# The end of a fused perceiver layer: a block closed without GpSimd's drain, and SyncE's last waits moved behind a branch

## The reference

```python
x = x + cross(layernorm(x), ctx_768)      # cosine of two projections, 256 wide
x = x + attention(layernorm(x))           # 16 heads of 16, each output freed of its share along v
x = x + experts(layernorm(x))             # top-1 of 14 experts, 256 -> 512 -> 256, gelu, times the probability
```

## Time and profile before

| what | value |
|---|---|
| median of three executions | 509.92 us (509.88 to 630.88) |
| span of the profiled execution | 518.2 us |
| instructions | 14215 |
| TensorE busy | 495.9 us, 96% of the span |
| GpSimd busy | 246.1 us, 47% |
| mean granted clock of TensorE | 0.992 |

### The profile page before, as it was taken

The page is one execution under the profiler, slowest core; times in us unless marked ns, Lnnn a source line. Parts: engine busy times, 40 slices in busy tenths (PEclk is TensorE's granted clock), DMA queues, the critical chain, the costliest instruction groups (busy, mean ns, idle before and its releaser), DMA issues.

```text
span 518.2 us, 14215 instructions
## 1 busy us (share of the span) xinstructions
PE 495.9 (96%) x4278; PEld 397.8 (77%) x4279; DVE 335.8 (65%) x1027; ACT 335.0 (65%) x814; POOL 246.1 (47%) x432
## 2 busy tenths in 40 slices
PE   8999999999999999999999999999879999999992
PEld 6545554667888888888888887778769999999992
DVE  4476665657889999888988899984632333323231
ACT  3766666589888988888888888764523333343430
POOL 2468665354334664655556555625443233333332
PEclk9999999999999999999999999999989999999998
DMA  8959995500002223222221122174545766666520
GB/s 302 311 173 282 304 259 172 168 1 3 2 2 72 67 74 92 92 51 88 92 92 46 46 63 69 44 250 145 183 167 186 220 208 209 220 192 212 187 82 8
DMA packets 35681, 70.41 MB, mean 136 GB/s; under 512 B 6752, under 2 KB 22242, under 8 KB 35632
## 3 DMA queue, kind: packets, MB, share of 16 engines
q1 hardware_dynamic: 31744, 60.72, 38.7%
q0 software_dynamic: 3456, 8.85, 4.5%
q10 hardware_dynamic: 432, 0.26, 0.2%
HBM read 58.93 MB, written 11.61 MB: 136 GB/s over the span
## 4 chain that ended last, share of the span: by engine, by line
PE 82%; DVE 5%; issue 4%; ACT 3%; POOL 2%; another core or an unknown queue 2%; DMA 1%; DVEq 0%; SPq 0%; POOLq 0%; ACTq 0%
PE psum L1520 11%; PE psum L1533 10%; PE psum L1446 9%; PE psum L1425 6%; PE psum L1404 6%; PE psum L1412 5%; PE psum L1475 5%; PE psum L1272 5%; PE psum L1372 5%; PE psum L1334 3%; PE psum L1343 3%; PE psum L1291 3%; PE psum L1294 3%; PE psum L1347 3%; PE psum L1312 2%
## 5 line engine op out<-in xcount | busy, mean ns | idle before, releaser
L1520 PEld LDWEIGHTS psum<-arena,ring 128*128 128x128 f32 x640 | 77.5, 192 | 4.6 <-ACT arena L1205 2.2
L1520 PE MATMUL psum<-arena,ring 128*128 128x128 f32 x640 | 78.5, 276 | 1.6 <-ACT arena L1205 1.5
L1533 PE MATMUL psum<-w_s,arena 128*128 x320 | 77.5, 386 | 0.0
L1205 ACT ACTIVATE arena<-psum 128x256 f32<-128x256 f32 x40 | 15.4, 385 | 94.0 <-PE psum L1272 53.0
L1021 DVE TENSOR_TENSOR arena<-psum,tok 128x256 f32<-128x256 f32 x40 | 17.0, 425 | 90.1 <-PE psum L1533 83.0
L1533 PEld LDWEIGHTS psum<-w_s,arena 128*128 128x128 f32 x320 | 58.7, 193 | 6.8
L545 POOL TENSOR_TENSOR ov<-o_n,v_s 128x256 f32<-128x256 f32 x32 | 26.1, 816 | 77.1 <-DVE o_n L785 77.1
L1171 ACT ACTIVATE arena<-kT,head_mask 128x256 f32<-128x256 f32 x128 | 59.3, 532 | 0.0
L603 POOL DMA_INDIRECT out<-arena,token_of x40 | 39.8, 996 | 19.7 <-POOL token_of L595 14.5
L1211 ACT ACTIVATE arena<-psum,b_s 128x128 f32<-128x128 f32 x160 | 45.6, 375 | 3.8 <-PE psum L1520 2.2
L892 DVE TENSOR_REDUCE smax<-psum 128x16 f32<-128x1024 f32 x32 | 39.1, 1222 | 11.4 <-PE psum L1425 11.3
(11 more groups left out here) (206 smaller groups left out, 1093.5 us busy)
## 6 DMA issues: line engine op xcount, KB each, us to landing
ring<-w SPq DMA_DIRECT2D x40, 512.0 KB, 3.6
w_s<-ctxT SPq DMA_DIRECT2D x15, 768.0 KB, 8.9
w_s<-w SPq DMA_DIRECT2D x16, 448.0 KB, 3.4
slot_rec<-routed SPq DMA_DIRECT2D x40, 132.0 KB
tok<-x SPq DMA_DIRECT2D x16, 256.0 KB, 8.2
w_s<-xT SPq DMA_DIRECT2D x12, 256.0 KB, 6.0
routed<-pad_rec SPq DMA_DIRECT2D x1, 1980.0 KB, 8.9
tok<-b SPq DMA_DIRECT2D x14, 128.0 KB
```

What stands on the lines that cost most here:

```text
L1520: mm = pe.matmul(hid_bank(p)[:, f * P:(f + 1) * P], w1_s[:, r, c * F + f * P:c * F + (f + 1) * P], xgT[:, p, c * P:(c + 1) * P], start=c = ...
L1533: mm = pe.matmul(bank(2 + q, D), hidT[:, q, f * P:(f + 1) * P], w2_s[:, bass.ds(e * (FC * D) + f * D, D)], start=f == 0, stop=f == FC - 1)
```

## The change

```diff
-        block = ctx.enter_context(nc.Block())
+        block = ctx.enter_context(nc.Block(no_gpsimd_drain=True))
...
+            def outputs_landed(slots):
+
+                for t in range(slots - 4, slots):
+                    sp.wait_ge(y_out[t % 4], arrivals(t, t % 4, 4, 16))
+
...
-                if isinstance(i, int) and i == part[1] - 1:
-
-                    for t in range(i - 3, i + 1):
-                        sp.wait_ge(y_out[t % 4], arrivals(t, t % 4, 4, 16))
+                if isinstance(i, int) and i == NSLOT - 1:
+                    outputs_landed(NSLOT)
...
             run_slots(sp, load_slot, 0, 0, used_tab, 1)
+            outputs_landed(EVEN)
```

## The result

The changed kernel takes 506.61 us (median of six executions, 506.08 to 506.88). The kernel before, beside it, takes 510.16 us (median of six; five lie between 509.88 and 510.24, one is the 630.88 us). 506.0 had been forecast. The medians differ by 3.5 us. The ratio is 0.9923, with a 95% interval of 0.991 to 0.9936, which stands for 3.9 us and 3.3 to 4.6. Run again on another chip with its variants, the changed kernel took 507.38 us against 510.64, ratio 0.9942 (0.9925 to 0.996).

What follows compares the result with a forecast made beforehand. Only the program's end was taken to matter, where the barrier waited for GpSimd's drain. 3.2 us from the drain and 0.7 from the branch made 3.9, so 509.92 - 3.9 = 506.0 us, with a range of 504.9 to 510.1.

Steps and rivals of the forecast that it cites:

- The view: End of the program: the closing line, not an average, shows the last 6.35 us, where nothing counts as busy.
- The drain, 3.2 us: Closing barrier: of GpSimd's 6.03 us drain, 2.8 us lie beside SyncE's wait and branch; removing it gains the exposed 3.2 us.
- The branch, 0.7 us, and nothing on its own: SyncE's load and branch after its last wait: moving the waits behind them gains 0.7 us, only with the drain gone.
- The small terms: Closing: 0.1 us from SyncE's last wait to its drain, 0.25 us for the new barrier (bounds 0.2 and 0.4).
- Carrying it over: From profiled execution to measured time: the 3.9 us was taken over as it is, 509.92 to 506.0 us.
- the 2% that I had set: Measured time: about 2% (10 us) was taken as what a measurement of this kernel can tell from no change.
- rival A: Behind the block: the drain's work comes back outside the span, or the option leaves the drain; 509.9 us, chance 0.16.
- the 8.3 us between span and median: Profiled execution: its span of 518.2 us stood 8.3 us above the median; the share due to profiling was left open.
- Rival C: Closing drain: long only because profiled, so less or only the branch's 0.7 us is gained; 506.8 to 509.2 us, chance 0.13.
- Rival B: Behind the block: winding-up starts only on request, and the closing there asks for it, taking 6.03 us; 512.2 us, chance 0.05.
- Rival D: Last outputs: they land sooner after issue when nothing is recorded; at most 6.0 us gained, 503.9 us, chance 0.05.

Runs made afterwards that it cites:

- the late drain: Kernel before, with GpSimd waiting for the last four outputs to land before its closing drain; 513.71 us against 510.57, ratio 1.0052.
- the kernel with the copy ahead of the wait: Changed kernel, with GpSimd copying the next slot's row numbers before waiting for output rows in slots 36 to 39; ratio to the kernel before 0.9946.
- the first four experiments: Variants of the kernel before: option alone (0.9951), moved waits alone (0.9999), one more drain ahead of the closing one (0.9999), GpSimd awaiting last outputs before draining (1.0052).
- the one with GpSimd's wait: Changed kernel, with GpSimd instead of SyncE waiting for the outputs of slots 36 to 39 to land; ratio to the kernel before 0.9932.

## Why the prediction was right

**The view.** The chain of waits ended at GpSimd's last scatter and showed nothing of the last 6.35 us. The closing line did, and all of the gain was in it. This held.

**The drain, 3.2 us.** Right in place and size: the option alone took the end of the span from 4.2 to between 1.1 and 1.2 us behind the last landing, where 3.1 had been expected of it, and 2.7 us off the median, with 1.7 to 3.3 inside its interval.

**The branch, 0.7 us, and nothing on its own.** Right. Moved alone it gave 0.9999; on top of the option the span's end drew in from 4.0 to 3.4 us behind the start of the last scatter. This is shown in the traces alone.

**The small terms.** I had 0.1 us from SyncE's last wait to its drain and 0.25 us for the barrier. It was 0.2 (504.2 to 504.4, one branch of 38 ns between) and 0.3 (504.4 to 504.7). The 0.25 us was charged for the new barrier, whose form no row of the kernel before shows; the changed kernel's closing has a drain on all engines but GpSimd as before, and one more semaphore instruction of 17 to 51 ns on each of the four. The last landing came 2.95 us after the scatter's start where it had been 3.05, which made up for most of it. So 3.9 us in the trace was right, partly by luck of 0.1 us or so, which is no more than these rows resolve.

**Carrying it over.** Here the sum had its largest error. I took 3.9 us over to the metric as it is. The new closing costs 0.3 us behind the span, which leaves 3.9 - 0.3 = 3.6 us. The medians differ by 3.5 us, but the interval of the ratio, 3.3 to 4.6 us, holds 3.6 and 3.9 alike (on the second chip 2.0 to 3.8). So the 0.3 us is shown by the time over the span, and that the medians come out at 3.5 us is no proof of it. The interval is 0.26% wide, so the measurement told this change of 0.8% from none, far less than the 2% that I had set. I had a doubt about it only under rival A, as a wait that comes back outside, all or nothing; it was 0.3 us, and of another kind.

**What the 8.3 us between span and median were.** Not the cost of being profiled, which I had left open. The metric is the span plus 1.8 us; the profiled execution was about 10 us slower than the usual one, nearly all of it in the two pieces shown above.

**Rival A** (509.9 us) falls, in its two forms. **Rival C** (the drain is shorter in the timed runs) falls too: the option alone brings 2.7 us. **Rival B** was half right. The winding-up does start only on request and takes its full length from there, as the late drain showed. But nothing behind the block requests it, since the time over the span is 2.0 to 2.1 us in the changed kernel with an explicit drain and without one. I had argued from the 4.0 us after the landing that there was a winding-up of the DMA work; it is there, but its clock is the number of scatters and not the landing. **Rival D** saw only the 0.1 us.

## What to carry to other kernels

Read the closing line of a program and set each engine's arrival against the others'; the chain of waits does not go there (here it had nothing of the last 6.35 us), and an engine's load and branch behind its last wait are worth something only when that engine comes last (ratio 0.9999 with the drain in place, 4.0 to 3.4 us in the traces without it). A drain of GpSimd cost 83 to 93 ns here for each scatter issued since the last one. It could be left out where SyncE waits for the data (2.7 us off the median), or split and put where GpSimd idles (a single execution of 506.82 us against a median of 510.4 beside it). Compare two traces only over the stretch that the change touches, and hold the rest against several executions.

## What the runs showed of the hardware

- GpSimd's drain took 83 to 93 ns for each indirect DMA of 128 rows issued since the last drain (25 to 72 of them), counted from when the engine had run out of other work. With 2 and 4 scatters behind the last drain it took 2.08 and 2.00 us and ended 0.1 and 0.2 us after SyncE's wait for the last landing (511.3 to 511.2 and 504.2 to 504.0). Right behind another drain it took 34 ns. No later wait for the winding-up of the 72 scatters was found: in the changed kernel the span ended 3.4 us after the start of the last scatter, and the time stood 2.0 to 2.1 us over the span with an explicit drain in it and without one.
- The last two scatters of the changed kernel, and those of the kernel with the copy ahead of the wait, started 0.80 or 0.81 us after the rows that they waited for were ready, whether or not another small operation stood between.
- The spread within a kernel (509.75 to 512.2 us for the kernel before) goes in part with TensorE's clock. Beside the first four experiments, its executions over 511 us had a mean clock of 0.990 to 0.992, those under 510 us 0.993 or 0.994. Two kernels with the same code up to the expert step, the changed kernel measured again and the one with GpSimd's wait, show it in the same stretch:

```profile
330.00:345.00 15.00, 13.35 (x151) 10.73 (x150) 12.34 (x37) 9.63 (x24) 5.39 (x9) 0.89 0.64 195
```

```profile
330.00:345.00 15.00, 13.31 (x162) 10.58 (x161) 13.11 (x41) 10.81 (x26) 5.75 (x10) 1.00 0.70 224
```

  At a granted clock of 0.89 on average, 151 matmuls are done in the 15 us, at 1.00 it is 162, and the last scatter starts at 502.02 in the one and at 500.82 in the other. It is not the whole of the spread: one execution of the changed kernel had a span of 507.7 us at a mean clock of 0.997. What sends the clock down in some executions and not in others stays open.
